# Graph layer kernel: inputs loaded from another queue and an earlier stage, and GpSimd's first norms placed between its gathers

## The reference

```python
xt = matmul(x, weight).reshape(-1, 4, 64)
alpha_l = einsum('ehd,hd->eh', xt[row], attn_l)      # row = src
alpha_r = einsum('ehd,hd->eh', xt[col], attn_r)      # col = dst
alpha = softmax(leaky_relu(alpha_l + alpha_r, 0.01), axis=1)
tmp = einsum('nh,nhd->nd', alpha[:n], xt[col[:n]])   # n = 6250
x = layernorm(x + broadcast(tmp over the 4 heads))
```

## Time and profile before

| | before |
|---|---|
| median of 3 runs | 2431.13 us (2417.94, 2431.13, 2432.23) |
| profiled execution, span | 2423.7 us |
| median of the runs less that span | 7.4 us |
| PE busy | 2208.4 us (91%) |
| DVE busy | 2146.6 us (89%) |
| ACT busy | 1930.8 us (80%) |
| POOL busy | 1714.9 us (71%) |
| gathers of the edge stage (L950) | 1568, 1539.2 us |

### The profile page before, as it was taken

How to read it: one execution, slowest core, us unless ns; L and a number is a source line. 1 busy time by engine, 2 the same in 40 slices (tenths; PEclk the granted TensorE clock), 3 DMA queues, 4 the chain that set the end, 5 groups by cost and what they waited for, 6 DMA issues and landing times. The chain is left out here.

```text
span 2423.7 us, 51960 instructions
## 1 busy us (share of the span) xinstructions
PE 2208.4 (91%) x12012; PEld 1805.3 (74%) x12012; DVE 2146.6 (89%) x6159; ACT 1930.8 (80%) x4051; POOL 1714.9 (71%) x1792
## 2 busy tenths in 40 slices
PE   6497799999999999999999999999999999999988
PEld 5254477787777878877877787878878877777766
DVE  5378699999999999999999999999999999999967
ACT  2465588888888888888888888888888888888866
POOL 1577477777777777777777777777777777777742
PEclk9798899999999999999999999999999999999999
DMA  8786699999999999999999999999999999999964
GB/s 255 193 204 201 234 283 275 267 278 277 281 274 277 277 280 282 283 271 273 282 273 273 277 278 279 283 278 280 276 273 280 281 279 274 280 276 278 272 195 174
DMA packets 349557, 642.53 MB, mean 265 GB/s; under 512 B 112156, under 2 KB 169872, under 8 KB 349528
## 3 DMA queue, kind: packets, MB, share of 16 engines
q0 software_dynamic: 129840, 418.60, 58.6%
q1 hardware_dynamic: 219688, 223.61, 32.4%
HBM read 583.26 MB, written 58.74 MB: 265 GB/s over the span
## 5 line engine op out<-in xcount | busy, mean ns | idle before, releaser
L950 POOL DMA_INDIRECT e_kv<-kv_tab,e_idx x1568 | 1539.2, 982 | 504.1 <-issue 417.6
L1078 ACT ACTIVATE e_gate_ps<-e_gate_ps 128x1024 f32<-128x1024 f32 x786 | 766.3, 1002 | 267.9 <-PE e_gate_ps L1010 267.3
L1150 DVE TENSOR_TENSOR e_gated<-e_kv,e_gate_ps 128x1024 f32<-128x1024 f32 x788 | 933.8, 1212 | 51.3 <-DMA e_kv<-kv_tab,e_idx 41.0
L997 PE MATMUL e_sum_ps<-e_gated,weighed_hot 128*128 128x256 f32 x3168 | 748.1, 379 | 2.1 <-ACT weighed_hot L1094 2.1
L1009 PE MATMUL e_gate_ps<-wd_hi_lo,high 128*128 128x512 f32 x1572 | 640.7, 408 | 115.6 <-DVE e_gated L1150 115.3
L997 PEld LDWEIGHTS e_sum_ps<-e_gated,weighed_hot 128*128 128x128 f32 x3168 | 599.5, 189 | 98.2 <-ACT weighed_hot L1094 2.7
L1010 PE MATMUL e_gate_ps<-wd_bias,low 128*128 128x512 f32 x1572 | 620.8, 395 | 0.0
L1159 DVE CUSTOM_DVE_ANT_0 e_gated<-e_gated,e_q_ps 128x256 f32<-128x256 f32 x1576 | 572.7, 412 | 0.0
L1094 ACT ACTIVATE weighed_hot<-hot,e_attn 128x128 f32<-128x128 bf16 x1580 | 520.4, 401 | 43.9 <-DVE e_attn L1169 35.5
L1009 PEld LDWEIGHTS e_gate_ps<-wd_hi_lo,high 128*128 128x128 f32 x1572 | 295.9, 188 | 250.8 <-DVE e_gated L1150 115.4
L1028 PE MATMUL e_q_ps<-q_win,hot_t 128*128 128x256 f32 x1572 | 423.5, 303 | 0.6 <-DVE e_dot L1159 0.6
(11 more groups left out here) (156 smaller groups left out, 1405.6 us busy)
## 6 DMA issues: line engine op xcount, KB each, us to landing
e_attr<-attr_groups_dram SPq DMA_DIRECT2D x784, 128.0 KB
e_q_next<-q_tab SPq DMA_DIRECT2D x98, 256.0 KB
e_kv<-kv_tab,e_idx POOLq DMA_INDIRECT x1568
sum_tab<-e_sums SPq DMA_DIRECT2D x100, 128.0 KB
e_prior<-sum_tab SPq DMA_DIRECT2D x99, 128.0 KB
kv_tab<-l_kv_out SPq DMA_DIRECT2D x49, 256.0 KB, 3.5
q_tab<-l_q_out SPq DMA_DIRECT2D x49, 256.0 KB, 2.9
sum_tab<-zeros SPq DMA_DIRECT2D x25, 256.0 KB, 2.6
```

What stands on the lines that cost most here:

```text
L950: pool.indirect_dma_start(kv[:, k, :], None, kv_tab, bass.IndirectOffsetOnAxis(ap=idx[:, k:k + 1], axis=0)).then_inc(kv_landed[k // G][k % ...
L997: last = nc.tensor.matmul(sum_ps[:, 0:H], weighed_hot[:, c % 2, k, :], gated[:, c * G + k, H:2 * H], start=(c == 0 and k == 0), stop=(c == ...
L1078: nc.scalar.activation(gate_ps[:, 2 * p:2 * p + 2, :], gate_ps[:, 2 * p:2 * p + 2, :], ACT.Silu).then_inc(silu_ready[s][p], 1)
L1150: nc.vector.tensor_tensor(gated[:, pair(s, p), :], kv[:, pair(s, p), :], gate_ps[:, 2 * p:2 * p + 2, :], ALU.mult).then_inc(gated_ready[s] ...
```

## The change

- `x_t` is issued by ScalarE, seven transfers ahead of everything else in its program. SyncE's queue has the weights and tables alone before the stores.
- x itself is loaded in the first stage by SyncE: 10 parts of 5 tiles, one behind every second pair stored, from the second pair on. The first stage waits for all of them before its end.
- `left_tab` and its 25 stores are gone. `by_src` gathers 32 bytes, all eight scores, out of `xt_tab` read as rows of eight numbers, with an index (`score_idx = idx * 33 + 32`) that VectorE computes in the first stage, after a wait for the index load.
- GpSimd does a first norm after the gather by destination of each tile from tile 25 on (`BEHIND = 25`), of the tile 25 earlier; the other 25 norms follow the last gather, each held until VectorE has weighed a number of tiles (`norms_paced`: 34 for the first, 49 for the last).
- All additions of half the bias are in the output stage, the first 12 without a wait (`BIASED = 12`).

The diff, without the changes of parameter lists that pass the new names:

```diff
@@ -31,7 +31,7 @@
 ACT = mybir.ActivationFunctionType
 AX = mybir.AxisListType
 EPS = 1e-5
-BIASED = 20
+BIASED = 12
 SLOPE = 0.01
 CUTOFF = 5.0
 
...
@@ -145,37 +145,40 @@
             b_ready, bias_done, bias_used, wd_rounded = (
                 sem(n) for n in ("b_ready", "bias_done", "bias_used", "wd_rounded"))
             PAIRS = range(0, TILES, 2)
             LOTS = LOT // 2
+            X_PARTS = [range(a, min(a + 5, TILES)) for a in range(0, TILES, 5)]
+            X_LOADS = sum(len({(t + 1) * P <= N for t in part}) for part in X_PARTS)
             stored = [sem(f"stored{j}") for j in range(LOTS)]
             projected, projected_copied = sem("projected"), sem("projected_copied")
 
             with nc.Block() as block:
                 @block.sync
                 def _(sp):
-                    def load(i):
-                        part = pieces[i]
-                        first, end = part[0] * P, min((part[-1] + 1) * P, N)
-                        sp.dma_start(x_t[:, :, first:end], x_turned[:, first:end].rearrange("(k p) n -> p k n", p=P)).then_inc(landed[i], 16)
+                    def load_x(part):
+                        whole = [t for t in part if (t + 1) * P <= N]
+                        if whole:
+                            sp.dma_start(x_sb[:, whole[0]:whole[-1] + 1, :],
+                                         x[whole[0] * P:(whole[-1] + 1) * P, :].rearrange("(i p) c -> p i c", p=P)).then_inc(x_landed, 16)
+                        for t in part:
+                            if t not in whole:
+                                sp.wait_ge(pad_zero, 2)
+                                sp.dma_start(x_sb[0:N - t * P, t, :], x[t * P:N, :]).then_inc(x_landed, 16)
 
                     sp.dma_start(w_ext[:, :, 0:H], weight.rearrange("(k p) n -> p k n", p=P)).then_inc(w_landed, 16)
                     sp.dma_start(attn[:, 0, :], attn_l.rearrange("h d -> (h d)").partition_broadcast(P)).then_inc(w_landed, 16)
                     sp.dma_start(attn[:, 1, :], attn_r.rearrange("h d -> (h d)").partition_broadcast(P)).then_inc(w_landed, 16)
-                    for i in range(len(pieces)):
-                        load(i)
-                        if i == 2:
-                            sp.dma_start(ln_cols[:, 0, :], ln_g).then_inc(ln_landed, 16)
-                            sp.dma_start(ln_cols[:, 1, :], ln_b).then_inc(ln_landed, 16)
-                            sp.dma_start(wqkv[:], wqkv_t.rearrange("(k p) n -> p k n", p=P)).then_inc(bias_landed, 16)
-                            sp.dma_start(bqkv_rep[:], bqkv.partition_broadcast(P)).then_inc(bias_landed, 16)
-                        if i == 3:
-                            sp.dma_start(dst_i[:], dst_tiles).then_inc(dst_landed, 16)
-                        if i == 4:
-                            sp.dma_start(dist[:], edge_weight_tiles).then_inc(dist_landed, 16)
+                    sp.dma_start(ln_cols[:, 0, :], ln_g).then_inc(ln_landed, 16)
+                    sp.dma_start(ln_cols[:, 1, :], ln_b).then_inc(ln_landed, 16)
+                    sp.dma_start(wqkv[:], wqkv_t.rearrange("(k p) n -> p k n", p=P)).then_inc(bias_landed, 16)
+                    sp.dma_start(bqkv_rep[:], bqkv.partition_broadcast(P)).then_inc(bias_landed, 16)
+                    sp.dma_start(dst_i[:], dst_tiles).then_inc(dst_landed, 16)
+                    sp.dma_start(dist[:], edge_weight_tiles).then_inc(dist_landed, 16)
                     sp.wait_ge(zero_ready, 1)
                     sp.dma_start(q_tab[TILES * P:NP, :], zeros[:]).then_inc(zeroed, 16)
                     for i, first in enumerate(PAIRS):
...
@@ -184,9 +187,13 @@
                         span = slice(first * P, (first + n) * P)
                         lot = slice(first % LOT, first % LOT + n)
                         sp.dma_start(xt_tab[span, :].rearrange("(i p) c -> p i c", p=P), xt_out[:, lot, :]).then_inc(stored[i % LOTS], 16)
-                        sp.dma_start(left_tab[span, :].rearrange("(i p) c -> p i c", p=P), xt_out[:, lot, H:H + HEADS]).then_inc(stored[i % LOTS], 16)
+                        if i % 2 and i // 2 < len(X_PARTS):
+                            load_x(X_PARTS[i // 2])
+                    for part in X_PARTS[len(PAIRS) // 2:]:
+                        load_x(part)
                     for j in range(LOTS):
-                        sp.wait_ge(stored[j], 32 * len(range(j, len(PAIRS), LOTS)))
+                        sp.wait_ge(stored[j], 16 * len(range(j, len(PAIRS), LOTS)))
+                    sp.wait_ge(x_landed, 16 * X_LOADS)
                     sp.wait_ge(zeroed, 16)
 
                 @block.gpsimd
...
@@ -222,12 +229,15 @@
 
                 @block.scalar
                 def _(act):
+                    for i, part in enumerate(pieces):
+                        first, end = part[0] * P, min((part[-1] + 1) * P, N)
+                        act.dma_start(x_t[:, :, first:end], x_turned[:, first:end].rearrange("(k p) n -> p k n", p=P)).then_inc(landed[i], 16)
                     nc.scalar.preload_act_table(ACT.Sin)
 
                     def copy_projected(t):
                         act.wait_ge(projected, t + 1)
                         if t >= LOT:
-                            act.wait_ge(stored[t % LOT // 2], 32 * (t // LOT))
+                            act.wait_ge(stored[t % LOT // 2], 16 * (t // LOT))
                         nc.scalar.copy(xt_out[:, t % LOT, :], xt_ps[:, t % SLOTS, 0:TAB]).then_inc(projected_copied, 1)
 
                     def round_weights():
...
@@ -310,6 +320,10 @@
                     for row in (64, 96):
                         nc.vector.memset(low[row:row + 1, :, :].bitcast(F32), 1.0)
 
+                    dve.wait_ge(small_landed, 16 * 4)
+                    nc.vector.tensor_scalar(score_idx[:], first_idx[:, 0, :], float(TAB // (2 * HEADS)), float(H // (2 * HEADS)),
+                                            ALU.mult, ALU.add).then_inc(score_idx_ready, 1)
+                    dve.wait_ge(score_idx_ready, 1)
                     dve.wait_ge(dst_landed, 16)
                     then(nc.vector.tensor_copy(dst_f[:], dst_i[:]))
                     by_block = dst_f[:].rearrange("p (b j) -> p b j", j=BLOCK_TILES)
...
-    xt_tab, left_tab, q_tab, kv_tab, sum_tab, zeros, TILES, TAB = (
...
@@ -472,45 +487,40 @@
         zeroed = sem("zeroed")
         blank = [range(a, min(a + 2, TILES + 1)) for a in range(0, TILES + 1, 2)]
 
-        def x_loads(g):
-
-            return len({(t + 1) * P <= x.shape[0] for t in chunk(g)})
+        BEHIND = DST_RING + 10
+
+        def norms_paced(u):
+
+            left = TILES - BEHIND
+            return min(TILES, TILES - DST_RING + (u + 1 - left) * DST_RING // (TILES - left))
 
         with nc.Block() as block:
             @block.gpsimd
             def _(pool):
+                def first_norm(u):
+                    g, i = CHUNK_OF[u], u - STARTS[CHUNK_OF[u]]
+                    pool.wait_ge(normed_ready, u + 1)
+                    nc.gpsimd.tensor_scalar(x_sb[:, u, :], x_sb[:, u, :], rstd[:, g, 0, i:i + 1], shift[:, g, 0, i:i + 1],
+                                            ALU.mult, ALU.add).then_inc(x1_ready, 1)
+
                 for g in range(CHUNKS):
                     for t in chunk(g):
-                        pool.indirect_dma_start(by_src[:, t, :], None, left_tab,
-                                                bass.IndirectOffsetOnAxis(ap=first_idx[:, 0, t:t + 1], axis=0)).then_inc(src_landed[g], 16)
+                        pool.indirect_dma_start(by_src[:, t, :], None, by_scores,
+                                                bass.IndirectOffsetOnAxis(ap=score_idx[:, t:t + 1], axis=0)).then_inc(src_landed[g], 16)
                     for t in chunk(g):
                         if t >= DST_RING:
                             pool.wait_ge(weighed_ready, t - DST_RING + 1)
                         pool.indirect_dma_start(by_dst[:, t % DST_RING, :], None, xt_tab,
                                                 bass.IndirectOffsetOnAxis(ap=first_idx[:, 1, t:t + 1], axis=0)).then_inc(dst_landed[g], 16)
-                for g in range(CHUNKS):
-                    for i, t in enumerate(chunk(g)):
-                        pool.wait_ge(normed_ready, t + 1)
-                        nc.gpsimd.tensor_scalar(x_sb[:, t, :], x_sb[:, t, :], rstd[:, g, 0, i:i + 1], shift[:, g, 0, i:i + 1],
-                                                ALU.mult, ALU.add).then_inc(x1_ready, 1)
-                        if t >= TILES - BIASED // 2:
-                            first = 2 * (t - TILES + BIASED // 2)
-                            pool.wait_ge(x1_ready, first + 2)
-                            for u in (first, first + 1):
-                                nc.gpsimd.tensor_tensor(x_sb[:, u, :], x_sb[:, u, :], bo_half[:], ALU.add).then_inc(biased, 1)
+                        if t >= BEHIND:
+                            first_norm(t - BEHIND)
+                for u in range(TILES - BEHIND, TILES):
```

(30 more changed lines are left out.)

17 lines of the change are left out of this document (9 added, 8 removed).

## The result

| | before | after |
|---|---|---|
| median, 8 runs each on one chip | 2422.38 us | 2439.1 us |
| ratio, 95% interval | | 1.0058 [1.0037, 1.0080] |
| profiled execution, span | 2423.7 us | 2438.8 us |
| first stage, to the first gather of layer 0 | 77.7 | 75.6 |
| layer 0 | 207.8 | 196.4 |

The change made the kernel slower by 0.58%, with an interval clear of no change, where I had it faster by 2.4 us (0.1%). The time lies in the forecast range, but that is partly luck: the range was laid around the three runs shown of before, with a median of 2431.13, and 31 runs of it, taken beside the first experiments, have 2423.81. The comparison with before is the measure, not the absolute time.

The account below looks back on a forecast made before the run. No engine was taken as near full in the early stages: DMA transfers and waits bound them, the edge stage standing untouched. First stage +3 and layer 0 -5.4 gave 2421.3, plus 7.4 to the median: 2429 us, range 2407 to 2440.

Parts of the forecast that it names:

- the sum: Whole kernel: first stage +3 and layer 0 -5.4 make -2.4 us on a span of 2423.7, so 2421.3.
- First stage, +3: First stage: 17.2 us more DMA work against 13.5 us of fillable idle time, so 3 us longer.
- the stall: First stage: ScalarE's 14.56 us wait for the first stored tiles to land, expected to go with loads by ScalarE's queue.
- Opening, 0: Layer 0's start: first score 3 us earlier without x in flight, lost again by chunk 6; 0 us.
- the 7.1 taken: Layer 0: 7.1 us assumed from a gather's issue to its use by the score.
- Norms between gathers, 11.7 us ahead at chunk 10: Layer 0: norms delay gathers by 0.54 us each, gather waits replace part of a VectorE stall; 11.7 us ahead of before.
- The run of 14, 7.6 us: Layer 0, behind the last gather: 14 norms in one piece keep VectorE out, losing 7.6 us.
- rival 1: Layer 0: VectorE gets in between GpSimd instructions, the norm burst costs 1 instead of 7.6 us; 2422 us, chance 0.2.
- Layer 0, −5.4: Layer 0 in all: 11.7 us won, 7.6 lost, 1.3 won from less lengthening; ends 5.4 us earlier.
- stall (c): Layer 0 of before: 37 GpSimd norms in one piece hold one VectorE operation for 19.07 us, about 18.9 us lost.
- Output, 0: Output stage: twenty bias additions moved there from layer 0 cost 0 us, up to 1 either way.
- Span to median, 7.4: Whole kernel: 7.4 us added from profiled span to median, taking 2421.3 to 2428.7.

Follow-up runs that it names:

- e6: Kernel before with one unused SBUF tensor of 49 columns, moving later tensors by 224 bytes, no instruction changed; 1.0060 of before.
- e13: Kernel before with an unused SBUF tensor of 256 bytes a partition at the index's place, no instruction changed; 0.9993 of before.
- e16: Changed kernel with only its last 25 norms held until VectorE has weighed 44 to 49 tiles, five norms for each; 1.0053 of before.
- e15: Changed kernel with the index tensor padded to a 256-byte shift and the last 25 norms held, x_t still by ScalarE; 0.9998 of before.
- e8: Changed kernel with the index tensor padded to a 256-byte shift and x_t loaded by SyncE in the old order; 0.9994 of before.
- e5: Changed kernel with the index tensor 64 columns wide instead of 49, a shift of 256 bytes; x_t still by ScalarE; 1.0039 of before.
- e2: Changed kernel with the seven x_t loads issued by SyncE again in the old order, index not padded; 1.0006 of before.
- e11: Changed kernel with padded index and x_t by SyncE, but one small load (ln_b) issued by ScalarE; 0.9985 of before.
- e3: Kernel before with one edit, the seven x_t loads issued by ScalarE; 1.0013 of before.
- e7: Kernel before with 32 unused bytes ahead of the edge stage's transfer targets and 32 behind, so these alone move; 1.0024 of before.
- e9: Kernel before with an unused SBUF tensor of 32 bytes a partition moving the tensors behind it, no instruction changed; 1.0026 of before.
- e10: Kernel before with an unused SBUF tensor of 128 bytes a partition moving the tensors behind it, no instruction changed; 1.0025 of before.
- e4: Kernel before with the change's norms between gathers and all bias additions in the output stage, nothing else; 0.9979 of before.
- e17: Changed kernel, padded index, last 25 norms held, the seven x_t loads in the change's new order but by SyncE; 0.9961 of before.

## Why the prediction was wrong

**The step that failed** is the first one: "The edge stage takes 2069 of 2424 us and no edit touches it". It set 2069 us aside at a price of nothing; in the profiled pair the stage took 28.8 us more. Ahead of it 13.5 us were won, some 7 if before's uncommonly long layer 0 is allowed for, so the sum's sign was lost here. Two edits touch it. A 196-byte tensor moves the targets of its loads off their multiples of 256 bytes (on the kernel before 0.60%, e6, and nothing at 256, e13; on the changed kernel with the norms held 0.55%, e16 to e15). And the seven loads of x_t by ScalarE cost 9 to 10 us in three pairs, by a mechanism that is open. Undoing both, e8 is at 0.9994, where the sum had put the whole at 0.999. How the loss of the change as it stands divides between the two is less clear, since they don't add up: taken off after, the padding gives 0.19% (e5) and x_t by SyncE 0.52% (e2), while on the kernel before the shift costs 0.60% and the loads 0.13%.

**First stage, +3:** −2.1 us. The stage's DMA work is 0.93 of 75 us, 69.8, so 11.3 were added to the 58.5 and not 17.2: x came cheaper than at the chosen 300 GB/s or the small stores had cost more than 3; the runs don't separate the two. The 5 us that I took as unfillable at the two ends had no row behind them; 5.2 us were idle. ScalarE's queue did not remove the stall, and the end of ScalarE's wait moved by only 1.15 us. e2, with x_t by SyncE, has a stage no longer (73.8 us), so the second queue brought nothing here. That both issuers share the same engines held: ScalarE's wait for the first store ended at 34.62 us with two queues and at 34.19 with one (e2).

**Opening, 0:** the first score waited 8.79 instead of 12.22 us; it stood 4.2 us behind its last gather's issue (79.61), less than the 7.1 taken, as the idle DMA engines were allowed to make it. It came 5.5 us earlier, 3.4 of them not from the first stage, against the 3 taken. Chunk 6 waited 1.92 us at 152.61 instead of 0.36, and stood 77.0 us into layer 0 instead of 75.9. All of it was given back, as forecast.

**Norms between gathers, 11.7 us ahead at chunk 10:** 229.50 to 215.63 is 13.9, of it 2.1 from the first stage, so 11.8. The number is right, with a price of 0.5 us a norm, and the score stood 6.96 us behind its last gather (208.67), near the 7.1. The way is less sure: I had VectorE waiting for gathers ahead of chunks 7 to 10, and the profile shows no such wait there. From chunk 6 on the scores come every 15.1 to 16.2 us instead of 14.5 to 14.6, with no idle time ahead of them. Whether the gathers set that pace, or the norms that lengthen VectorE's operations, is not shown.

**The run of 14, 7.6 us:** its length was right, its effect comes both ways: rival 1 held in after and four more, the forecast in e8 and e11. From one row of 37 norms I had taken that VectorE never gets in.

**Layer 0, −5.4:** −11.4 in the profiled pair. But the 207.8 of before is a long one: the unchanged layer 0 took 196.3 to 202.9 in e3, e6, e7, e9, e10 and e13. Against their middle of 201.0 the change wins some 5 us, about what e4 measures (0.21%, 5 us). The 18.9 us of stall (c) were partly an accident of one execution: at the place of its 19.07 us operation e3, e6, e7 and e10 have one of 10.8 to 13.1 us beside the run of norms, and e9 and e13 none, but one of 6.19 us later.

**Output, 0:** 69.2 against 69.4; the additions by GpSimd, 24 in one run, began with its first instruction. **Span to median, 7.4:** the profiled execution of after took 2440.66 us, 1.9 over its span, and its median of 8 runs is 0.3 over it. The 7.4 were the scatter of three runs.

## What to carry to other kernels

- "No edit touches this stage" holds for its instructions, not for its addresses. Where a loop lives by transfers, compare the start of every SBUF target before and after, modulo 256, and pad a small new tensor so that they keep their places. A control kernel with an unused tensor and no other edit tells what the move alone costs.
- Undo each suspect edit alone and all together, on the changed kernel and on the kernel before. Here the same shift was worth 0.60, 0.19, 0.12 and 0.55% in four settings, and one pair would have misled.
- A stall seen in one execution is one draw. Where a run of operations on one engine can hold an operation of another, price it by several executions, and order the work so that the long run does not start when the other's critical operation is due.

## What was not expected of the hardware

- Rows of 2 KB into SBUF took 120.0 ns with their targets 224 bytes off, against 116.5, and that alone cost a kernel at 0.94 DMA share 0.60%.
- 6.4 MB in seven loads through a second issuing queue, landed by 36 us, cost 9 to 10 us in three pairs, with the queue idle afterwards; the same loads in the same order by SyncE cost nothing (e17), one small load on that queue did not either (e11), and on the kernel before they cost at most 0.3% (e3).
- The same run of 14 or 15 GpSimd norms held one VectorE operation for 7.3 to 7.6 us in two executions and let VectorE through in five.
